# Experts' second product with tokens on partitions: a one-core transformer block on Trainium2

## The reference

```
q, k, v = x@Wq+bq, x@Wk+bk, x@Wv+bv                    # token mixing
h = prelu(((d_gamma * (q @ k.T)) @ v) @ Wo + bo)
h = h + attention(layernorm(h))                        # 8 heads of 8, softmax with a bias by position, projection
xn = layernorm(layernorm(h)) * gamma + beta            # experts
logits = xn @ Wr + br                                  # 8 experts
w = softmax over the two largest logits, 0 for the others
y = sum over e of w[:, e] * (gelu(xn @ W1[e] + b1[e]) @ W2[e] + b2[e])     # W1[e] 64x128, W2[e] 128x64
out = h + y
```

## Time and profile before

| | us |
|---|---|
| median of 3 runs | 570.92 (570.85 to 572.3) |
| the profiled execution | 577.15 |
| its span, first to last instruction | 575.4 |
| PE busy | 532.8 (93%) |
| DVE busy | 459.9 (80%) |
| ACT busy | 354.0 (62%) |
| POOL busy | 80.0 (14%) |
| mean granted TensorE clock | 0.946 |

### The profile page before, as it was taken

The page is one execution under the profiler, slowest core; times in us unless marked ns, Lnnn a source line. Parts: engine busy times, 40 slices in busy tenths (PEclk is TensorE's granted clock), DMA queues, the critical chain, the costliest instruction groups (busy, mean ns, idle before and its releaser), DMA issues.

```text
span 575.4 us, 12945 instructions
## 1 busy us (share of the span) xinstructions
PE 532.8 (93%) x4230; PEld 183.5 (32%) x4234; DVE 459.9 (80%) x542; ACT 354.0 (62%) x624; POOL 80.0 (14%) x180
## 2 busy tenths in 40 slices
PE   7979998665999999999999999999998988999996
PEld 5232333131233333333333333333332532232221
DVE  2646596979799999999999999999999466775653
ACT  1000122231788888888898988889897455445442
POOL 9600110111301010010100001010001340210100
PEclk9968999955899999999999999999999789999999
DMA  7900078393122323232222323232243000100000
GB/s 273 233 13 1 1 213 227 117 241 110 40 73 82 81 79 80 58 89 71 82 78 71 83 59 88 72 83 77 70 131 94 12 9 12 41 0 20 18 19 18
DMA packets 51095, 46.33 MB, mean 81 GB/s; under 512 B 26265, under 2 KB 39034, under 8 KB 51066
## 3 DMA queue, kind: packets, MB, share of 16 engines
q1 hardware_dynamic: 51066, 45.94, 29.1%
HBM read 29.75 MB, written 16.17 MB: 80 GB/s over the span
## 4 chain that ended last, share of the span: by engine, by line
PE 68%; DVE 4%; DMA 1%; issue 1%; ACT 1%; SPq 1%; DVEq 0%; ACTq 0%
PE ps L1398 25%; PE ps L1310 13%; PE ps L1383 13%; PE ps L1535 5%; PE ps L1561 5%; PE ps L1415 2%; DVE nmax L868 2%; PE ps L1387 1%; PE ps L1324 1%; PE ps L1548 1%; DVE probs L1142 1%; PE ps L1440 1%; DMA maxima<-max_t 1%; SPq L413 1%; PE ps L1428 0%
## 5 line engine op out<-in xcount | busy, mean ns | idle before, releaser
L724 ACT ACTIVATE probs<-ps 128x512 f32<-128x512 f32 x512 | 278.1, 596 | 65.4 <-PE ps L1383 55.6
L868 DVE TENSOR_REDUCE nmax<-ps 128x1 f32<-128x1024 f32 x256 | 302.0, 1218 | 19.7 <-PE ps L1310 10.3
L1398 PE MATMUL ps<-probs,v_ring 128*32 128x256 f32 x2048 | 166.4, 398 | 0.0
L1310 PE MATMUL ps<-k_ring,q_ring 48*128 48x512 bf16 x512 | 103.3, 400 | 6.6 <-DVE nmax L868 6.6
L1383 PE MATMUL ps<-q_ring,k_ring 51*128 51x512 bf16 x512 | 104.0, 389 | 5.5 <-DMA q_ring<-maxima 1.5
L1310 PEld LDWEIGHTS ps<-k_ring,q_ring 48*128 48x128 bf16 x512 | 24.9, 94 | 113.6 <-issue 99.9
L1398 PEld LDWEIGHTS ps<-probs,v_ring 128*32 128x32 f32 x2048 | 40.7, 108 | 62.6 <-issue 37.7
L1142 DVE TENSOR_TENSOR probs<-probs,ps 128x1024 f32<-128x1024 f32 x32 | 39.0, 1220 | 25.3 <-PE ps L1548 19.9
L743 ACT ACTIVATE probs<-ps,wide_w 128x1024 f32<-128x1024 f32 x32 | 35.3, 1114 | 33.6 <-PE ps L1535 31.5
L889 DVE SCALAR_TENSOR_TENSOR gated<-ps,v_s,gamma_sb 128x1024 f32<-128x1024 f32 x32 | 40.6, 1280 | 15.5 <-PE ps L1232 15.4
L582 POOL TENSOR_TENSOR max_p<-nmax,zeros 128x8 bf16<-128x8 f32 x32 | 6.5, 202 | 284.1 <-DVE nmax L868 260.6
(11 more groups left out here) (162 smaller groups left out, 344.0 us busy)
## 6 DMA issues: line engine op xcount, KB each, us to landing
k_ring<-qk_parts SPq DMA_DIRECT2D x64, 96.0 KB, 2.4
q_ring<-qk_parts SPq DMA_DIRECT2D x64, 96.0 KB, 2.3
gamma_sb<-gamma_t SPq DMA_DIRECT2D x4, 1024.0 KB, 10.5
v_padded<-v_pad SPq DMA_DIRECT2D x4, 1024.0 KB, 4.8
v_ring<-v_padded SPq DMA_DIRECT2D x32, 128.0 KB, 3.2
outputs<-o_t SPq DMA_DIRECT2D x32, 128.0 KB
qk_parts<-qk_h SPq DMA_DIRECT2D x8, 384.0 KB, 4.3
x_ring<-bias_parts SPq DMA_DIRECT2D x32, 96.0 KB, 3.1
```

The costliest lines, as they stand in the source:

```text
L724: A.activation(probs[:, s % 4, HALF * j:HALF * (j + 1)], ps[:, key_bank(s, j), :], ACT.Exp).then_inc(exp_done[j], 1)
L868: V.tensor_reduce(nmax[:, par, s:s + 1], ps[:, bank:bank + 2, :].rearrange("p a n -> p (a n)"), AX, ALU.max, negate=True).then_inc(s1_redu ...
L1310: return mm(ps[:, bank + j, :], q_ring[rows, u, P * s:P * (s + 1)], k_ring[rows, u, HALF * j:HALF * (j + 1)], start=True, stop=(s > 0 or j ...
L1398: last = mm(ps[VC * j:VC * (j + 1), PVB, 0:2 * P], v_ring[:, u, m, :], probs[:, m % 4, 2 * P * j:2 * P * (j + 1)], start=(m == 0), stop=(m ...
```

## The change

In the expert stage `down(k)` turns round: the gelu output is the stationary operand, 128 tokens at a time, and W2[e] the moving one with 64 columns, eight products for a unit. The result has tokens on partitions, so the routing weight is one number for a partition and token tile: VectorE multiplies the 128x512 result with it out of PSUM (`weigh`), and GpSimd adds it up (`add_up`), beginning with the residual. `spread`, `pick`, the multiplication of the hidden layer, `finish` and the residual at the end go. `hid` has four buffers. The b2 term is a product of its own in bank 6 (`weigh_b2`, 12 bfloat16 products for a batch), which VectorE adds once for a batch (`add_b2`). The last unit is done in halves, with both steps on VectorE.

The logits are made with tokens on partitions, stationary xn and a moving table `wr_d` of 16 columns (Wr twice, block diagonal, written by two small ScalarE copies in token mixing); `logits_copy` and `turn_logits` go. `project_attention` of batches 0 to 2 takes the lower and upper rows in turn, into two banks, without the wait between. The small tables are made in five pieces, after steps 5 and 6 of batch 0 and 0, 1 and 2 of batch 1. The places of the stages in the tables `WITHIN` move.

```diff
+        hid = probs
+        weighed = gated[:, :, :].rearrange("p a (i n) -> p (a i) n", n=HALF)
...
+        def out_bank(k, m):
+            return 6 if k == UNITS - 1 and m >= NT // 2 else 4 + k % 2
...
-            for j in range(2):
-                for i in range(PARTS):
-                    after(ones_where(pick[:, :, :], -UPPER * j - E * i, [[-1, E], [0, HID]], 1))
...
+            def add_up(k):
+                b, e = k // E, k % E
+                total = out_s[b % 2][:, :, :].rearrange("p (c j) d -> p c j d", j=2)
+                new = weighed[:, k % 4, :].rearrange("p (c j d) -> p c j d", j=2, d=D)
+                old = total
+                pool.wait_ge(out_weighed, k + 1)
+                if e == 0:
+                    old = h_all[:, NT * b:NT * (b + 1), :].rearrange("p (j c) d -> p c j d", j=2)
+                    if b >= 2:
+                        pool.wait_ge(out_stored[b % 2], 16 * 2)
+                else:
+                    pool.wait_ge(out_summed, b * (E - 1) + e)
+                if e == E // 2:
+                    pool.wait_ge(b2_added, b + 1)
+                last = gp.tensor_tensor(total, new, old, ALU.add)
+                if e == E - 1:
+                    last.then_inc(out_ready, 1)
+                else:
+                    last.then_inc(out_summed, 1)
...
+            WITHIN = {E - 1: (scale_attention, B - 1), E + 2: (late_norm, B - 1), 2 * E + 1: (exp_gap, 2)}
...
+                        rows = slice(UPPER * j, UPPER * (j + 1))
+                        A.activation(wr_d[rows, E * j:E * (j + 1)], up_w[rows, UPS:UPS + E], ACT.Copy).then_inc(wr_ready, 1)
                 if b >= 1:
                     square(b - 1)
...
                 act.wait_ge(up_done, k + 1)
-                if k >= 2:
-                    act.wait_ge(hid_scaled, k - 1)
+                if k >= RING:
+                    act.wait_ge(down_done, k - 3)
...
-            def small_tables():
+            step = chain(dve_seq, 0)
+            def bias_high():
                 dve.wait_ge(aug_loaded, 3 * 16)
                 V.tensor_scalar(qkv_w[:, 0:D], qkv_w[:, 0:D], SCALE, None, ALU.mult).then_inc(qk_scaled, 1)
                 dve.wait_ge(small_loaded, 3 * 16)
                 dve.wait_ge(pads_ready, 1)
-                step = chain(dve_seq, 0)
                 step(V.tensor_scalar(f_diff[:, P:P + RPB], rpb_s[:, :], rpb_s[:, 0:1], None, ALU.subtract))
+            def bias_middle():
                 step(V.tensor_copy(f_p[:, 0, :], f_diff[:, :]))
                 step(V.tensor_tensor(f_rest[:, :], f_diff[:, :], f_p[:, 0, :], ALU.subtract))
+            def bias_low():
                 step(V.tensor_copy(f_p[:, 1, :], f_rest[:, :]))
                 V.tensor_tensor(f_p[:, 2, :], f_rest[:, :], f_p[:, 1, :], ALU.subtract).then_inc(f_ready, 1)
...
+            def b2_parts(j):
+                rows = slice(UPPER * j, UPPER * j + PARTS * E)
+                p0, p1, p2 = (b2_p[rows, i, j, :] for i in range(PARTS))
+                step(V.tensor_copy(p0, b2_r[rows, :]))
+                step(V.tensor_tensor(b2_rest[rows, :], b2_r[rows, :], p0, ALU.subtract))
+                step(V.tensor_copy(p1, b2_rest[rows, :]))
+                V.tensor_tensor(p2, b2_rest[rows, :], p1, ALU.subtract).then_inc(b2_ready, 1)
...
-                        small_tables()
+                        bias_high()
+                    if b == 0 and s == 6:
+                        bias_middle()
+                    if b == 1 and s == 0:
+                        bias_low()
+                    if b == 1 and s in (1, 2):
+                        b2_parts(s - 1)
...
+                if b < B - 1:
+                    h_v = h_b.rearrange("p (j c) d -> p j c d", j=2)
+                    V.tensor_tensor(h_v, h_v, ps[:, 2:4, 0:HALF // 2].rearrange("p j (c d) -> p j c d", d=D),
+                                    ALU.add).then_inc(res_seq, 1)
...
+            def logits_bias(b):
+                dve.wait_ge(routed, b + 1)
+                V.tensor_tensor(lg[:, NT * b:NT * (b + 1), :],
+                                ps[:, 7 if b == B - 1 else 0, D * b:D * (b + 1)].rearrange("p (m e) -> p m e", e=E),
...
-                V.tensor_tensor(hid_w[:, k % 2, :], hid[:, k % 2, :],
-                                ps[:, 4:6, :].rearrange("p a n -> p (a n)"), ALU.mult).then_inc(hid_scaled, 1)
+            def weigh(k, cols):
+                b, e = k // E, k % E
+                V.tensor_tensor(weighed[:, k % 4, D * cols.start:D * cols.stop].rearrange("p (m d) -> p m d", d=D),
+                                ps[:, out_bank(k, cols.start), D * cols.start:D * cols.stop].rearrange(
+                                    "p (m d) -> p m d", d=D),
+                                w_full[:, NT * b + cols.start:NT * b + cols.stop, e:e + 1].to_broadcast(
+                                    [P, cols.stop - cols.start, D]), ALU.mult).then_inc(out_weighed, 1)
...
+            def add_b2(b):
+                dve.wait_ge(b2_summed, b + 1)
+                dve.wait_ge(out_summed, b * (E - 1) + E // 2)
+                total = out_s[b % 2][:, :, :].rearrange("p m d -> p (m d)")
+                V.tensor_tensor(total, total, ps[:, 6, :], ALU.add).then_inc(b2_added, 1)
...
+            WITHIN = {2: [(two_weights, 1)], 3: [(invert_sums, B - 1)], 5: [(all_weights, 1)], 6: [(route_parts, 1)],
+                      E + 2: [(add_residual, B - 1), (center, B - 1)], E + 3: [(variance, B - 1)],
+                      E + 4: [(scale, B - 1)], 2 * E: [(logits_bias, B - 1), (first_choice, 2)],
+                      2 * E + 1: [(second_top, 2), (second_choice, 2)], 2 * E + 4: [(two_weights, 2), (all_weights, 2)],
+                      2 * E + 5: [(route_parts, 2)]}
...
+                if b < B - 1:
                     for c in range(NT // 2):
-                        rows, m = slice(D * j, D * (j + 1)), NT // 2 * j + c
-                        last = mm(ps[:, proj_bank(b), D * m:D * (m + 1)], ao_all[rows, b, P * c:P * (c + 1)],
-                                  proj_s[rows, :], start=True, stop=True)
-                    if j == 0:
-                        last.then_inc(proj_half, 1)
-                        pe.wait_ge(proj_half, b + 1)
+                        for j in range(2):
+                            rows = slice(D * j, D * (j + 1))
+                            last = mm(ps[:, 2 + j, D * c:D * (c + 1)], ao_all[rows, b, P * c:P * (c + 1)],
+                                      proj_s[rows, :], start=True, stop=True)
...
-                pe.wait_ge(up_loaded, 16)
+                pe.wait_ge(wr_ready, 2)
                 pe.wait_ge(xf_ready, b + 1)
-                bank = (0, 3, 3, 7)[b]
-                for j in range(2):
-                    t, rows = j + (2 if b == 2 else 0), slice(UPPER * j, UPPER * (j + 1))
-                    last = mm(ps[VC * t:VC * (t + 1), bank, :], up_w[rows, UPS:UPS + VC], xf[rows, b, :],
+                if b < B - 1:
+                    pe.wait_ge(lg_read, b)
+                for c in range(NT // 2):
+                    first = D * b + 2 * E * c
+                    last = mm(ps[:, 7 if b == B - 1 else 0, first:first + 2 * E], xf[:, b, P * c:P * (c + 1)], wr_d[:, :],
                               start=True, stop=True)
...
-                b, e = k // E, k % E
-                pe.wait_ge(hid_scaled, k + 1)
-                if e == 0:
-                    pe.wait_ge(ye_copied, b)
+                e = k % E
+                pe.wait_ge(gelu_done, k + 1)
+                if k >= 2:
+                    pe.wait_ge(out_weighed, k - 1)
+                for m in range(NT):
+                    first = HALF * (m % 2) + P * (m // 2)
+                    if k == UNITS - 1 and m == NT // 2:
+                        pe.wait_ge(b2_added, B)
+                    last = mm(ps[:, out_bank(k, m), D * m:D * (m + 1)], hid[:, k % RING, first:first + P], w2_s[:, e, :],
+                              start=True, stop=True)
+                    if k == UNITS - 1 and m == NT // 2 - 1:
+                        last.then_inc(down_done, 1)
+                last.then_inc(down_done, 1)
+            def weigh_b2(b):
+                pe.wait_ge(w_t_copied, b + 1)
+                pe.wait_ge(b2_added, b)
+                for c in range(NT // 2):
                     for i in range(PARTS):
-                        mm(ps[:, 6, :], b2_p[:, i, :, :].rearrange("p j d -> p (j d)"), wt[:, b, :],
...
+                        last = mm(ps[:, 6, P * c:P * (c + 1)], wt[:, b, P * c:P * (c + 1)],
+                                  b2_p[:, i, :, :].rearrange("p j d -> p (j d)"), start=(i == 0), stop=(i == PARTS - 1))
+                last.then_inc(b2_summed, 1)
...
-            WITHIN = {E - 1: (turn_weights, 1), E: (project_attention, B - 1), E + 1: (finish, 0),
-                      E + 4: (turn_norm, B - 1), E + 5: (logits, B - 1), E + 7: (turn_logits, 2),
-                      2 * E + 1: (finish, 1), 2 * E + 4: (turn_weights, 2), 3 * E + 1: (finish, 2)}
```

(3 more changed lines are left out.)

229 lines of the change are left out of this document (72 added, 157 removed).

## The result

The changed kernel takes 612.1 us in the median of 4 executions (604.8 to 616.6), the kernel before 571.6: a ratio of 1.064, 95% interval 1.052 to 1.077. All ratios here compare only executions within 1.5% of their kernel's fastest (616.6 is left out of this one), while medians and lists hold every execution. The prediction had said 573.5 us with a range to 583. The side was right, the size wrong by 39 us.

What follows compares the result with a forecast made beforehand. TensorE was taken as the bound, busy 93% of the span; token mixing -7.5, last round -7 and expert stage +17.1 gave +2.6 us, so the median goes from 570.92 to 573.5 us, range 566 to 583.

Steps and rivals of the forecast that it cites:

- +17.1: Expert stage: us added behind the end of the first down product, all at full clock.
- Rival 2: Expert stage: the clock falls for 13.7 us, costing 6.8 us, total 580 us; chance 0.15.
- the cut: End of the first down product, where the prediction split the time; 84.5 us stood behind it in the kernel before.
- 101.6: Predicted us from the end of the first down product to the kernel's end after the change.
- units 9 to 11: Expert stage: where down, turned weights, batch 3's projection and b2 meet, and the clock might fall.
- The wait at unit 22: Expert stage: TensorE waits for batch 3's routing weights ahead of turn_weights(2), 1.8 us (0 to 2.5).
- The bounds 1.01 and 2.77: Down in us per unit: 1.01 if loads hide behind columns, 2.77 if they take turns; forecast 1.79.
- rivals 4 and 5: Down's loads: hidden, down near 1.01, total 549 us; or in series, down 2.77, 604 us; chance 0.05 each.
- Token mixing: Smaller table pieces remove TensorE's wait near 29 us and the clock fall, retain(9) earlier: -7.5 us.
- Last round: Attention's end: projections of 1.1 us and shorter routing, -10.9 us at full clock, -7 with one fall.
- Rival 1: Clock never falls in token mixing or the last round: 569.6 us, or 567 with luck; chance 0.28.
- Rival 3: Last round: routing gets no shorter, only 3 of the 10.9 us come, 577.5 us; chance 0.09.

Runs made afterwards that it cites:

- e5: Changed kernel with the sums of units 20 and 21 made on VectorE behind route_parts(2) instead of on GpSimd; 616.7 us.
- e8: Changed kernel with turn_weights(2) in unit 24 and down products of 32 columns instead of 64; 612.6 us.
- e10: Changed kernel with turn_weights(2) in unit 24 and TensorE stopped ahead of down(13) and down(21), 1.8 to 2.0 us each; 628.0 us.
- e4: Changed kernel with turn_weights(2) and weights_copy(2) in unit 24 instead of 22; 588.7 us.
- e11: Changed kernel with turn_weights(2) in unit 24 and four unused 512-column products, two ahead of turn_norm(0), two ahead of up(2); 579.0 us, ratio to before 1.009.
- e12: e3 plus unused 512-column products, two ahead of turn_norm(0) and one ahead of up(1); 560.4 us, ratio to before 0.977.
- e1: Kernel before with only the small tables cut into five pieces; 570.55 us, ratio 0.997.
- e3: Kernel before with the changed tables, projections and logits, but the old expert stage; 564.2 us, ratio 0.987.
- e13: e10 with four unused 512-column products behind each stop and behind the wait for the first gelu; 595.9 us.
- e14: e12 plus unused products between the first attention scores and ahead of each project_vv; 562.0 us, ratio to before 0.977.

## Why the prediction was wrong

- **The step that failed: the expert stage was taken at full clock.** The sum has +17.1 for it, and measured was +41.8. Rival 2 had the right event, "a fall of 13.7 us, as long as those seen, costs half of it, 6.8". Its size and its number were the mistake, and with them the chance of 0.15. In the changed kernel behind the cut 45 us run at half clock (483.5 to 497.8 and 562.6 to 593.4), which is some 22 of the 24.7 us by which 126.3 is above 101.6. The length of 13.7 was carried over from the last round, where products of 256 and 512 columns stand between the small ones; in e5, e8 and e10 it is 55 to 68. And it wasn't "as long as those seen": slices 9 to 11 of the earlier trace rows are one of 34 us:
```profile
115.00:148.00 33.00, 22.09 (x113) 8.05 (x113) 26.07 (x27) 10.36 (x18) 8.16 (x13) 0.50 0.55 154
```
The argument against the rival, "between them always stands an up of full columns", fell too: up stands in every unit of the stretches of 55 to 68 us. Why a stretch lasts 17 us in one execution and 68 in another stays open.
- **Its start was put in the wrong place.** I looked at units 9 to 11, where small products meet. They kept the clock in the profiled execution; its stretches began behind waits. The wait at unit 22 was predicted as 1.8 us and priced at its own length. It was 3.3 us (two additions of GpSimd held VectorE up, 2 us that I had called hidden after looking only at who waits for GpSimd), and with what it set off it cost 18 us (e4). The wait of 1.6 us ahead of turn_norm(0) has the same in it: hn took VectorE 1.52 us in the changed kernel, beside GpSimd's square of 1.04, and 0.68 in the kernel before.
- **The sum at full clock was right.** e11's profiled execution has no fall behind the cut and no wait at unit 22: its first down ends at 476.52, the span is 578.3, so 101.8 us stand behind the cut; 101.6 predicted. That they agree this well is in part luck, since misses cancel inside: down 1.93 in place of 1.79 (+4.3 for 31), the 1.8 us wait moved out, b2 products at 0.67 us a batch in place of 1.02 (-1.4), and 0.9 that I can't place. e12, whose expert stage is the old one at full clock, has 558.4 - 474.55 = 83.9 behind it, so the new stage costs 17.9 us more than the old at full clock; +17.1 predicted. The first down in both, e11's first (start us, us):
```profile
474.59 1.93 PE ps L1572 x16
```
```profile
473.54 1.01 PE ps L1563 x4
```
- **Loads: the pace was right, the seams were missing.** Records follow each other at 0.112 us as forecast, and 16 of them are 1.79; a unit has 0.14 us more between up and down, which I took for nothing. The bounds 1.01 and 2.77 stand far off, and with them rivals 4 and 5. The rule of the Trainium skill, "TensorE: Matmul & The Clock Gate", Part 3, that a load runs beside a product only on another row group isn't borne out: these loads use all 128 rows, and 32 columns fewer in each product leave the pace at 0.112 us (e8).
- **Token mixing: right for the trace, wrong for the median.** Retain(9) moved from 46.46 to 40.91, with a start 2.1 us later, so -7.65 against -7.5. But e1 moves the median by 2 us. By the clocks, the profiled execution was 1.1% above the median because of this very fall, and I scaled it down instead of taking that fall out of the sum first. What the usual execution has to gain there is 2 us, or nothing. So this term alone made the forecast some 5 us too low, and e11's executions at the highest clock (.975) took 575.6 to 577.7 us, not 573.5.
- **Last round: the chain was right, the clock not.** Projections take 1.11 us for 16 records, as predicted. From the first of them to up(0) I had 24.6 us at full clock; e12, at full clock, takes 24.9 (442.16 to 467.04), with two products in it where TensorE stood still. With a fall I had 28.6; the changed kernel took 32.7, with a stretch of 20.5 us.
- Rival 1 fell with the expert stage. Rival 3 fell by e12's 24.9 us, where the kernel before took 34.1, and by the 8 us that e3 keeps.

## What to carry to other kernels

A short wait of TensorE has two prices: its own length, and half of the stretch at half clock that it may set off. The second can't be read from one stretch: with the new stage's products behind the wait they lasted 3.4 to 68 us here, or didn't come, so a range has to hold the longest seen in any row of the trace, and more than one. With full products right behind the same waits they lasted 3.4 us at most, and e13 took 32 us less than e10, with all its executions within 8 us. And before a sum is made against a profiled execution, compare its clock with that of the usual ones.

## What was new about the hardware

- TensorE is busy in 67.94 of 68.00 us at a granted clock of 0.50 (e8), and the same code then runs 56 us at 1.00: e10, with twice the columns, has a stretch of the same length. Executions of one kernel took 576 and 636 us, at mean clocks of .975 and .871 (e11).
- Float32 weights of 128 columns and 128 rows: a record every 0.112 us at full clock, whether 32 or 64 columns follow (down 1.90 and 1.93 us).
- A VectorE operation of 128x8 with both inputs in SBUF takes 1.10 us beside GpSimd's addition of 1.27 us that began 0.18 us ahead of it, and 0.17 us without.
- Half clock where TensorE waits for VectorE costs next to nothing: e12 has 27 us of it from 110 us on and takes 558.0 to 560.5 us at a mean clock of 0.975, e14 without it takes 559.0 and 559.4 at 0.999.
